# Two-block adaLN transformer on one core: gate rows through DRAM and partition-broadcast loads in place of TensorE products, gated operands in PSUM, the shared expert first in layer 0

## The reference

```python
# layer 0: 8 routed experts of width 256, one shared, the best two weighted by their probability
router_probs = softmax(flat @ router_w + router_b)
topk_probs, topk_idx = top_k(router_probs, 2)
weights = zeros_like(router_probs).at[arange(T)[:, None], topk_idx].add(topk_probs)
shared_out = gelu(flat @ sw1 + sb1) @ sw2 + sb2
h1 = gelu(einsum('td,edh->teh', flat, rw1) + rb1[None])
expert_out = einsum('teh,ehd->ted', h1, rw2) + rb2[None]
mixed = einsum('ted,te->td', expert_out, weights)
return shared_out + mixed
# layer 1: 8 routed experts of width 176, one shared with a sigmoid gate sg
combine = sum(one_hot(topk_i, 8) * (topk_w / sum(topk_w))[..., None])
eo = einsum('eti,eih->eth', silu(x @ w_gate) * (x @ w_up), w_down)
out = einsum('te,eth->th', combine, eo) + sg * ((silu(x @ sw_gate) * (x @ sw_up)) @ sw_down)
```

## Time and profile before

| | |
|---|---|
| median of 3 runs | 516.86 us (512.07 to 517.73) |
| profiled execution | 514.67 us, its span 512.6 us |
| TensorE busy | 446.7 us (87%) |
| VectorE busy | 372.4 us (73%) |
| ScalarE busy | 347.5 us (68%) |
| GpSimd busy | 265.7 us (52%) |
| granted clock, mean | 0.845 |

### The profile page before, as it was taken

The page is one execution under the profiler, slowest core; times in us unless marked ns, Lnnn a source line. Parts: engine busy times, 40 slices in busy tenths (PEclk is TensorE's granted clock), DMA queues, the critical chain, the costliest instruction groups (busy, mean ns, idle before and its releaser), DMA issues.

```text
span 512.6 us, 7844 instructions
## 1 busy us (share of the span) xinstructions
PE 446.7 (87%) x2247; PEld 288.5 (56%) x2268; DVE 372.4 (73%) x920; ACT 347.5 (68%) x905; POOL 265.7 (52%) x287
## 2 busy tenths in 40 slices
PE   3799869979789799969999785979899999999995
PEld 2577757657467467643444232334367776767673
DVE  5665886676997878599678963986756759667663
ACT  2557647778767767779988893979745565565542
POOL 3440647786766667722343541435338646455553
PEclk9999978999999999985555555555589999999999
DMA  7700000000024524322265254100110000000000
GB/s 190 214 1 1 1 1 1 1 1 1 0 63 70 69 63 88 62 63 85 44 106 121 65 77 110 40 2 20 23 21 0 2 1 20 1 2 20 1 20 22
DMA packets 32642, 21.75 MB, mean 42 GB/s; under 512 B 3677, under 2 KB 31781, under 8 KB 32600
## 3 DMA queue, kind: packets, MB, share of 16 engines
q1 hardware_dynamic: 32600, 21.25, 19.3%
HBM read 14.95 MB, written 6.29 MB: 41 GB/s over the span
## 4 chain that ended last, share of the span: by engine, by line
PE 32%; DVE 17%; issue 5%; ACT 3%; DMA 2%; POOL 0%; POOLq 0%; SPq 0%; DVEq 0%; ACTq 0%
PE P L1406 7%; PE P L1144 5%; PE P L1146 5%; PE P L1396 5%; PE P L1145 5%; DVE nm L810 4%; DVE tmp L873 2%; DMA attention_rows<-O 2%; DVE SC L534 2%; DVE tmp L880 1%; ACT EX L1079 1%; PE P L1243 1%; DVE kvs L630 1%; PE P L1274 1%; PE P L1483 1%
## 5 line engine op out<-in xcount | busy, mean ns | idle before, releaser
L397 POOL TENSOR_TENSOR hidl<-tmp,hidh 128x512 fp32r<-128x512 f32 x116 | 149.0, 1289 | 101.0 <-ACT hidh L1024 98.4
L1079 ACT ACTIVATE EX<-P,nm 128x256 f32<-128x256 f32 x256 | 117.3, 499 | 21.8 <-DVE nm L810 21.7
L1024 ACT ACTIVATE hidh<-tmp 128x512 fp32r<-128x512 f32 x116 | 73.3, 631 | 51.2 <-DVE tmp L773 23.9
L810 DVE TENSOR_REDUCE nm<-P 128x4 f32<-128x1024 f32 x64 | 77.9, 1219 | 21.8 <-PE P L1396 21.4
L1406 PE MATMUL P<-EX,qs 128*32 128x256 f32 x512 | 68.1, 630 | 19.3 <-DVE O L825 19.1
L1144 PE MATMUL P<-XH,WH 128*128 128x512 f32 x176 | 76.9, 437 | 0.9 <-DVE O L825 0.6
L1146 PE MATMUL P<-XL,WH 128*128 128x512 f32 x176 | 70.7, 402 | 0.0
L441 POOL TENSOR_TENSOR qs<-qT,rz 128x128 f32<-128x128 f32 x64 | 24.5, 404 | 88.7 <-DVE rz L818 88.7
L1145 PE MATMUL P<-XH,WL 128*128 128x512 f32 x176 | 70.4, 400 | 0.0
L1144 PE MATMUL P<-hidh,WH 128*128 128x512 f32 x124 | 63.6, 513 | 5.6 <-POOL hidl L397 4.3
L773 DVE TENSOR_TENSOR tmp<-wmod,P 128x512 f32<-128x512 f32 x64 | 43.4, 684 | 27.1 <-ACT wmod L1050 19.1
(11 more groups left out here) (149 smaller groups left out, 725.8 us busy)
## 6 DMA issues: line engine op xcount, KB each, us to landing
kv_parts<-kvs SPq DMA_DIRECT2D x16, 256.0 KB, 2.3
VS<-kv_parts SPq DMA_DIRECT2D x48, 64.0 KB
KS<-kv_parts SPq DMA_DIRECT2D x48, 64.0 KB
X<-in_x SPq DMA_DIRECT2D x4, 256.0 KB, 5.0
stage<-in_L_ffn_rw SPq DMA_DIRECT2D x1, 1024.0 KB, 5.9
attention_rows<-O SPq DMA_DIRECT2D x32, 32.0 KB
SC<-attention_rows SPq DMA_DIRECT2D x8, 128.0 KB, 2.1
out<-X SPq DMA_DIRECT2D x4, 256.0 KB, 2.3
```

Source lines behind the costliest of these rows:

```text
L397: nc.gpsimd.tensor_tensor(hidl[:, u % 3, :], source, hidh[:, u % 3, :].bitcast(fp32), ALU.subtract).then_inc(s["low_ready"], 1)
L810: v.tensor_reduce(nm1[:, g % 4, 2 * h:2 * h + 2, :], P[:, bank:bank + 2, :].rearrange("p j (h s) -> p (j h) s", h=2), AX.X, ALU.max, negat ...
L1024: sc.activation(hidh[:, u % 3, :], source, ACT.Copy).then_inc(s["high_ready"], 1)
L1079: last = sc.activation(ex1(g, j)[:, h * S:(h + 1) * S], P[:, bank_s1(g, j), h * S:(h + 1) * S], ACT.Exp, bias=nm1[:, g % 4, j, h:h + 1], a ...
```

## The change

W, no longer split, is transposed in fp32 and copied by ScalarE to WT [9, 2, 512]. SP stores it to a DRAM tensor (`gates_store`, gate_rows), and loads each expert's row of 512 tokens to all 128 partitions of G, a ring of GR = 4 tiles (`gate_load`). In layer 1 a step may span two experts and then has two loads for parts of the partitions. The selector products, their selectors, identb, dbp and the splits go. Gelu is written in place into the bank of the up product, of which there are now five (u % 5), and VectorE multiplies bank x G. In layer 1 act x u is written to u's bank, and multiplied from there by G; g and u have three banks each. The shared expert, which has no gate, is steps 0 and 1 of a pair in place of 16 and 17 (`block0`). `router_weights` has three parts, behind steps 9, 10, 11 in layer 0 and 6, 7, 8 in layer 1, and `weights_back` stands at step 12 (16 before) and 9 (11 before). The bias product is one fp32 product after the second down step. On SP the K/V stores come in halves, and the K/V loads of pairs 0 and 1 in quarters between gate loads.

```diff
 
-        N_LD = {"ld_c": 3, "ld_m1": 2, "ld_b": 9, "ld_w0": 7, "ld_f0": 4, "ld_w1": 6, "ld_r1": 2}
+        def block0(i):
+
+            return (i + E * C0) % STEPS0
...
+        def gates_loaded(q):
+
+            return 16 * sum(gate_loads(m) for m in range(q % GR, q + 1, GR))
+
+        def gates_used(q):
+
+            return C0 * (q + 1) if q < NP * E else NP * E * C0 + q - NP * E + 1
```

SP's new functions and its order in layer 0:

```diff
+            def gates_store(n):
+
+                sp.wait_ge(s["wt_sb"], n + 1)
+                sp.dma_start(scratch["gw"][n, 0:E + n // NP, :], WT[0:E + n // NP, n % 2, :]).then_inc(gw_out, 16)
+
+            def gate_load(q):
+
+                if q < NP * E:
+                    n, first = q // E, q % E == 0
+                else:
+                    n, first = NP + (q - NP * E) // C1, (q - NP * E) % C1 == 0
+                if first:
+                    sp.wait_ge(gw_out, 16 * (n + 1))
+                if q >= GR:
+                    sp.wait_ge(s["bc_read"], gates_used(q - GR))
+                if q < NP * E:
+                    sp.dma_start(G[:, q % GR, :], scratch["gw"][n, q % E, :].partition_broadcast(D)
+                                 ).then_inc(gate_in[q % GR], 16)
+                    return
+                i = (q - NP * E) % C1
+                for e in experts_of(q - NP * E):
+                    lo = max(e * H1 - i * D, 0)
+                    hi = min((e + 1) * H1 - i * D, D) if e < E else D
+                    sp.dma_start(G[lo:hi, q % GR, :], scratch["gw"][n, e, :].partition_broadcast(hi - lo)
+                                 ).then_inc(gate_in[q % GR], 16)
...
+            for e in range(GR):
+                gate_load(e)
+            for p in range(NP):
+                if p >= 2:
+                    kv_store(p - 2, 1)
+                for e in range(GR, E):
+                    gate_load(p * E + e)
+                    if p >= 2:
+                        kv_load(p - 2, [e - GR])
+                if p + 1 < NP:
+                    gates_store(p + 1)
+                    for e in range(GR):
+                        gate_load((p + 1) * E + e)
+                if p >= 1:
+                    kv_store(p - 1, 0)
```

VectorE and ScalarE:

```diff
-                    link(v.tensor_tensor(W[:, ts, 0:E], oh[:, ts, 0, :], oh[:, ts, 1, :], ALU.add))
-                    link(v.tensor_copy(WP[:, ts, 0:n9], W[:, ts, 0:n9]))
-                if part == 3:
-                    link(v.tensor_tensor(res[:, ts, 0:n9], W[:, ts, 0:n9], WP[:, ts, 0:n9], ALU.subtract))
-                    link(v.tensor_copy(WP[:, ts, n9:2 * n9], res[:, ts, 0:n9]))
-                    v.tensor_tensor(WP[:, ts, 2 * n9:3 * n9], res[:, ts, 0:n9], WP[:, ts, n9:2 * n9],
-                                    ALU.subtract).then_inc(s["w_ready"], 1)
+                    v.tensor_tensor(W[:, ts, 0:E], oh[:, ts, 0, :], oh[:, ts, 1, :], ALU.add
+                                    ).then_inc(s["w_ready"], 1)
...
-                if i < E * C0:
-
-                    dve.wait_ge(s["bc_ps"], p * E + i // C0 + 1)
+                if i >= C0:
+                    q = p * E + i // C0 - 1
+                    dve.wait_ge(gate_in[q % GR], gates_loaded(q))
...
                         dve.wait_ge(s["low_ready"], u - 3)
-                    v.tensor_tensor(hidf0[:, u % 4, :], act_out[:, u % 3, :], P[:, bank_bc(p * E + i // C0), :],
+                    v.tensor_tensor(hidf0[:, u % 4, :], P[:, bank_up(u), :], G[:, q % GR, :],
                                     ALU.mult).then_inc(s["bc_read"], 1)
...
-                    if i in (9, 12, 13, 14):
-                        router_weights(0, p + 1, (9, 12, 13, 14).index(i))
+                    if i in (9, 10, 11):
+                        router_weights(0, p + 1, i - 9)
...
-                v.tensor_tensor(gu[:, n % 2, :], act_out[:, n % 3, :], P[:, bank_u(n), :], ALU.mult
+                v.tensor_tensor(P[:, bank_u(n), :], act_out[:, n % 3, :], P[:, bank_u(n), :], ALU.mult
                                 ).then_inc(s["u_read"], 1)
...
+                q = NP * E + n
+                dve.wait_ge(gate_in[q % GR], gates_loaded(q))
                 if n >= 2:
...
+                v.tensor_tensor(hidf[:, n % 2, :], P[:, bank_u(n), :], G[:, q % GR, :],
                                 ALU.mult).then_inc(s["bc_read"], 1)
                 if p in (1, 2):
...
-                    if i in (6, 8, 9, 10):
-                        router_weights(1, p + 1, (6, 8, 9, 10).index(i))
+                    if i in (6, 7, 8):
+                        router_weights(1, p + 1, i - 6)
...
-                if u >= 3:
-
-
-                    pp, ii = divmod(u - 3, STEPS0)
-                    if ii < E * C0:
-                        act.wait_ge(s["bc_read"], pp * E * C0 + ii + 1)
-                    else:
-                        act.wait_ge(s["low_ready"], u - 2)
-                sc.activation(act_out[:, u % 3, :], P[:, bank_up(u), :], ACT.Gelu,
-                              bias=ub0[:, i // C0, i % C0:i % C0 + 1]).then_inc(s["act_ready"], 1)
+                e, c = divmod(block0(i), C0)
+                if i < C0 and p >= 1:
+                    act.wait_ge(s["low_ready"], (p - 1) * STEPS0 + C0)
+                sc.activation(act_out[:, u % 3, :] if i < C0 else P[:, bank_up(u), :], P[:, bank_up(u), :], ACT.Gelu,
+                              bias=ub0[:, e, c:c + 1]).then_inc(s["act_ready"], 1)
```

TensorE:

```diff
-                    for n in range(3):
-                        mm(P[:, bank_y0[p], :], dbp[:, n, :], WPT[:, p % 2, :], start=(n == 0), stop=False)
                 pe.wait_ge(s["high_ready"], u + 1)
                 pe.wait_ge(s["low_ready"], u + 1)
-                last = split_mm(bank_y0[p], (STEPS0 + i) * D, D, hidh[:, u % 3, :], hidl[:, u % 3, :],
-                                False, i == STEPS0 - 1)
+                last = split_mm(bank_y0[p], (STEPS0 + block0(i)) * D, D, hidh[:, u % 3, :], hidl[:, u % 3, :],
+                                i == 0, i == STEPS0 - 1)
                 last.then_inc(s["down_done"], 1)
+                if i == C0:
+
+                    pe.wait_ge(s["wt_sb"], p + 1)
+                    mm(P[:, bank_y0[p], :], db0[:, :], WT[0:E, p % 2, :], start=False, stop=False)
...
-                claim(bank_up(u), "act_ready", u + 1)
-                split_mm(bank_up(u), i * D, D, XH[:, p % 2, :], XL[:, p % 2, :], True, True
+                if i < C0:
+                    claim(bank_up(u), "act_ready", u + 1)
+                else:
+                    claim(bank_up(u), "bc_read", p * E * C0 + i - C0 + 1)
+                split_mm(bank_up(u), block0(i) * D, D, XH[:, p % 2, :], XL[:, p % 2, :], True, True
                          ).then_inc(s["up_ps"], 1)
                 if u == 1:
                     weights_back(0, 0)
-                if i == 0 and p >= 1 or u == 2:
-                    pe.wait_ge(s["wt_sb"], p + 1)
-
-
-                for e in [0, 1] if u == 2 else [i // C0] if i % C0 == 0 and 0 < u and i < E * C0 else []:
-                    m = p * E + e
-                    claim(bank_bc(m), "bc_read", (m + 1) * C0)
-                    mm(P[:, bank_bc(m), :], sel0[:, e * D:(e + 1) * D], WPT[:, p % 2, :],
-                       start=True, stop=True).then_inc(s["bc_ps"], 1)
...
-                claim(bank_u(n), "u_read", n + 1)
+                claim(bank_u(n), "bc_read", NP * E * C0 + n + 1)
...
-                if i == 0:
-                    pe.wait_ge(s["wt_sb"], NP + p + 1)
-                claim(bank_bc(n), "bc_read", NP * E * C0 + n + 1)
-                mm(P[:, bank_bc(n), :], sel1[:, i * D:(i + 1) * D], WPT[:, p % 2, :], start=True, stop=True
-                   ).then_inc(s["bc_ps"], 1)
                 if n >= LAG:
...
 
 def bank_up(u):
-    return u % 3
-
-
-def bank_bc(m):
-    return 3 + m % 2
...
 
 def bank_g(n):
-    return n % 2
+    return (0, 1, 4)[n % 3]
 
 
 def bank_u(n):
-    return (2, 6)[n % 2]
+    return (2, 6, 3)[n % 3]
```

141 lines of the change are left out of this document (66 added, 75 removed).

## The result

The changed kernel takes 525.84 us (median of 4 runs, 522.13 to 529.71), beside 515.95 us for the kernel before in the same comparison (median of 4, 512.07 to 517.73). The ratio is 1.0203 with a 95% interval of 1.0107 to 1.0298: it is slower by 1 to 3%, and outside the forecast range. The profiled execution took 522.13 us for a span of 520.2, at a mean clock of 0.823 (0.845 before).

What follows compares the result with a forecast made beforehand. TensorE was taken to bound layer 1 throughout and layer 0 only between its waits; -9.6 - 1.3 - 2.4 - 2.8 + 3.0 = -13.1 us from 514.67 gave 501.6, stated as 502 us, range 495 to 508.

Steps and rivals of the forecast that it cites:

- the moved order: Layer 0: weights due on TensorE at step 12, not 16, make its waits for W longer; +3.0 us (0 to +8).
- the start of layer 0: Layer 0's start: TensorE resumes 0.84 us earlier, shared expert covers the gates' DRAM trip; -1.3 us (-2 to +2).
- the first rival: VectorE's lag eats more: W late in all three layer 0 pairs, layer 1 loses 2 us; 509 us, chance 0.22.
- Less 1.5 because VectorE is then ahead when kvs is due: Layer 0, within the +3.0 us: earlier weights leave VectorE ahead for kvs, taking 1.5 us off.
- Layer 0's other products: Layer 0 after the start: 28 products go (-6.4), less 2.5 behind waits, 1.0 bias, 0.45 transposes; -2.4 us.
- VectorE's split: Layer 0: the missing split of the weights gives 1.4 us in each pair where TensorE waits for VectorE; -2.8 us.
- Layer 1, forecast -9.6 us: Layer 1 experts: 52 products go (-12.0), +1.4 longer waits, +0.5 fp32 transposes, +0.5 a late gate.
- SP: SP's queue in both layers: gates are loaded far enough ahead of other stores and loads; cost put at nothing.
- the third rival: Gate loads come one at a time, pacing layer 1 at 2.7 us per gate; 523 us, chance 0.08.
- The second (decoupling): Rival: five Gelu banks and no split remove low-part and kvs waits, reordering costs nothing; 494 us, chance 0.17.
- the signs I named for being wrong: VectorE waits for G repeatedly, ScalarE or VectorE pay for PSUM writes, or the layer 0 stage grows.
- PSUM as output: ScalarE's Gelu and VectorE's multiply writing PSUM: no change taken, times within 0.05 us of 684 ns.

Runs made afterwards that it cites:

- filled: The changed kernel with 14 throw-away bf16 products ahead of each later TensorE wait for W: 519.65 us, ratio 1.011 to the kernel before.
- late_both: The changed kernel with the routing weights' steps put back to their old places in both layers: 507.29 us, ratio 0.992 to the kernel before.
- kv_order: late_both with VectorE's b1kt rows moved to pair 1's step 1 and the last pair's second K/V product one step later: 505.05 us, ratio 0.983.
- first_gates_free: late_both with the first four gate rows loaded early from an input (pair 0's first four experts get wrong gates): 501.39 us, ratio 0.982.
- extra_products: late_both with one more bf16 product, overwritten afterwards, in each of layer 1's 52 chunks: 516.08 us, ratio 1.008.
- no_gate_loads: The changed kernel with only the first four gate rows loaded, later gate stores and loads left out (wrong gates): 526.22 us, ratio 1.025.
- combined: late_both with the changes of bias_first and kv_order together: 503.25 us, ratio 0.987.
- no_bias: late_both without layer 0's four fp32 bias products (routed experts' down biases missing): 499.26 us, ratio 0.976.
- bias_first: late_both with each pair's fp32 bias product issued ahead of the waits of the first gated down product: 505.93 us, ratio 0.989.
- before_early: The kernel before with only layer 0's routing weights moved early: 525.22 us, ratio 1.026.

## Why the prediction was wrong, step by step

By spans, the changed kernel is 7.6 us longer where the sum says 13.1 less, a miss of 20.7 us: 19.5 in layer 0 (+16.0 for -3.5), 3.3 in layer 1, less 2.1 in attention. The experiments put some 9.6 of it on the moved order (5.3 in layer 0, 4.3 in layer 1), some 5 on the start of layer 0 and some 4 on the waits for kvs; these shares may overlap, each is known to 2 or 3 us, and the rest is open.

**The moved order, forecast +3.0 us (0 to +8), is the largest step that failed.** The waits were forecast well. TensorE's first W wait came at 74.08 in place of 75.33; the next was 2.94 us (forecast 2.3 to 4.3), then 4.08 and 4.07 (2.8 to 6.5). What failed is the price that I put on them. I charged only the growth of each wait, and left out the clock behind it: 3.7 us by filled. I named that drop, but as part of the first rival, for "a wait near 5 us"; it came behind each wait of 2.9 to 4.1. And of the waits "in place of 2.0" I took the old SC and low-part waits as gone: the SC waits fell from 3.6 us to 1.3, but just ahead of two of the W waits TensorE now waits 1.4 us for a low part (at 134.9 and 180.8), where the longest was 0.8 before. Undone in the changed kernel the order gives 8.3 us in layer 0 and 4.3 in layer 1; done alone in the kernel before it costs 14.2.

**"Less 1.5 because VectorE is then ahead when kvs is due" did not come.** The kvs waits went from 2.7 us to 6.0. They are 6.5 in late_both, so the order itself took off 0.5 us, and something else in the change added 3.8, for which I had no term. kv_order's 4.3 us say what the place of VectorE's K/V work is worth.

**The start of layer 0, forecast -1.3 us (-2 to +2), failed too.** From the Gelu of step 0 to that of step 9 the kernel before takes 22.3 us and the changed one 26.1, so +3.8. The trip was right to 0.4 us: first gated down product forecast at 83.7, measured at 83.35. But TensorE ran out of other work at 81.4 and not at 83.4: I had counted products as half clocked until about 80, where they were so only until 77, and I had counted the bias product into the cover, where it stands behind the first gated product. The wait of 1.98 us then dropped the clock, for which I had no price: first_gates_free measures +7.0 us for the trip in late_both, +4.0 once the bias product is moved.

**Layer 0's other products, forecast -2.4 us.** One term in it, +1.0 for the bias product, was mis-sized. The length of the product itself was nearly right (1.05 against 0.94) in three pairs, but 2.00 in pair 0, where it stands directly behind the first wait. Leaving it out gives 8.8 us, placing it ahead of the wait 5.9.

**VectorE's split, forecast -2.8 us.** VectorE's busy time fell by some 7 us in the changed kernel, but by only 1 in late_both (115.3 against 116.1). The split is gone in both; the 24 operations that make SC take 636 ns each before, 539 in the changed kernel and 747 in late_both, so the busy time tells mostly where they stand. No run separates the split, so the term is open.

**Layer 1, forecast -9.6 us.** The changed kernel gained 6.3. With the old order it gained 10.6: the sum was near, its parts less so. The products give 8.0 rather than 12.0 - 1.4 = 10.6 (extra_products); the other 2.6 us are of banks in place, deeper rings or the split, not separated. The early order, for which I put nothing here, takes 4 to 7 us back.

**SP and the third rival.** SP at nothing held: no_gate_loads. The rival that gave the nearest time, 523, is wrong as a mechanism. VectorE waited for G once, 4.8 us at 80.5, and 256 KB landed in a median of 3.2 us with several loads in flight. I had forecast under 3.

**The first rival, 509 by VectorE's lag, is the one that held in kind**: the waits at three pairs and the one-step distance in layer 1 (W waits of 4.1 and 2.8 us there, 6.8 in all; it priced them at 2). It added 5 for layer 0's late end, but the W waits themselves never came late; their price did. The second (decoupling) did not come: it has the waits for low parts and kvs go, 3.1 and 2.7 us, and they are 5.9 and 6.0 in the changed kernel and 8.2 and 6.5 in late_both, where the reordering costs nothing.

**The signs and the range.** Of the signs I named for being wrong one came, that the layer 0 stage grows. TensorE is busy for 88% of the last stage (119.0 of 135.7 us) and 91% in late_both, where I said over 94%: with the products gone, the waits weigh more. The range does not follow from its terms: with both at their ends (-9 and -12, or +2 and -6) it is 494 to 511 and not 495 to 508. 525.84 is outside of both.

**PSUM as output** changes little, as forecast. Gelu into PSUM takes 660 ns and into SBUF 686 in the same stage, the act x u multiply into PSUM 693 and the multiply by G into SBUF 691 in layer 1 (groups of instructions: count, busy, mean ns):

```profile
L1094 ACT ACTIVATE P<-P,ub 128x512 f32<-128x512 f32 x64 | 42.2, 660 | 23.2 <-PE P L1190 23.1
...
L1094 ACT ACTIVATE wmod<-P,ub 128x512 f32<-128x512 f32 x8 | 5.4, 686 | 1.7 <-PE P L1190 1.7
```

```profile
L928 DVE TENSOR_TENSOR P<-wmod,P 128x512 f32<-128x512 f32 x52 | 36.0, 693 | 29.8 <-ACT wmod L1157 28.0 <-PE P L1190 1.5
L936 DVE TENSOR_TENSOR tmp<-P,G 128x512 f32<-128x512 f32 x52 | 35.9, 691 | 4.1 <-POOL hidl L463 2.4
```

The page "ScalarE: Activation LUTs" of the Trainium skill (section Step-by-step: what each stage is for) says that PSUM is the faster destination for ScalarE; the 26 ns agree.

## What to carry to other kernels

When a producer chain is moved, ask first where the consumer asks for it: on an engine that works in order, a request made before the producer is done is a wait for everything behind it, and here, four steps early in layer 0 and two in layer 1, it turned a gain of 0.8% into a loss of 2%. Price a TensorE wait of some 2 us and up as the wait and, with the chances listed below, the half-clocked products behind it, and put slow products inside a wait rather than directly behind one. Compare single stages before whole times: where a neighbouring stage varies by 7 us between kernels that share it, only the stage shows a share of 4.

## What the runs showed of the hardware

- Over the expert stages of the 16 traces, the mean granted clock in the 4 us behind a TensorE wait was at most 0.67 for all 33 waits of 3.6 to 5.9 us, 0.50 to 0.68 for 15 of the 26 waits of 2.3 to 3.1 us and 1.00 for the other 11, 0.54 to 0.60 for 11 of the 13 waits of 1.8 to 2.3 us, and 1.00 for 56 of the 61 waits of 1.3 to 1.7 us. The same wait of 2.4 us for kvs was followed by half clock in six kernels (at 202 us in the changed one) and by full clock in four (at 196 us in late_both).
- So the length of a wait does not settle it between 1.4 and 3.1 us. Behind 3.04 us in combined (first row) the clock was 1.00, where it was 0.60 to 0.68 behind 3.05 and 3.06 us in three others; behind 1.42 us in no_bias (second row) it was 0.57:

```profile
147.40:151.40 4.00, 4.00 (x18) 3.31 (x19) 2.62 (x8) 1.96 (x3) 0.66 (x1) 1.00 0.42 120
...
131.20:135.20 4.00, 3.99 (x13) 2.93 (x13) 3.90 (x11) 3.04 (x7) 2.51 (x2) 0.57 0.00 0
```

- Behind the wait of 2.0 us that ended at 83.35 in the changed kernel the products had full spacing for 0.5 us first (0.31 and 0.23 us between starts); in bias_first they were 0.43 apart from 84.21 on.
- It stayed low for longer where the fp32 bias product (8 rows by 512) came next: 0.67, 0.50 and 0.55 over 84 to 96 us in late_both; without it, or with it ahead of the wait, products were back to full spacing at 88.2.
- The same attention stage took 142.3 to 149.7 us in the 16 kernels, with a granted clock of 0.57 in the shortest and 0.52 in the longest; before_early's 144.2 us had 0.52 too, so the clock is not all of it.
- 14 MB moved in layer 0's stage of the changed kernel, 83 GB/s; with the gates behind the first four left out it was 39 GB/s, and the stage was no shorter (no_gate_loads).
